# Flamingo cross-attention and expert block: whole turns of three angle chunks by matmuls, weight splits one unit later

## What is computed

```python
x = x + tanh(g_xattn) * xattn(layernorm(x), ctx, Wq, Wk, Wv, Wo, q_norm_w, k_norm_w, pos_ctx, pos_x)
x = x + tanh(g_ffn)   * ffn(layernorm(x), w_router, w_gate, w_up, w_down, ws_gate, ws_up, ws_down)
```

```python
inv_freq = 1.0 / 10000 ** (arange(0, 128, 2) / 128)
freqs = pos[..., None] * inv_freq                    # 64 angles for each position
x * cos(freqs, freqs) + rotate_half(x) * sin(freqs, freqs)
```

## Time and profile before

| | us |
|---|---|
| median of 3 runs | 1235.36 |
| lowest and highest run | 1235.15, 1236.42 |
| profiled execution | 1235.88 |
| span of its trace | 1234.10 |
| TensorE busy in the span | 1198.6 |
| DVE, ACT, POOL busy | 1015.6, 885.7, 925.6 |

### The profile page before, as it was taken

One profiled execution on the slowest core, in us unless ns is written; L12 is line 12 of the kernel. 1 busy time (PEld: TensorE's weight loads), 2 busy tenths in 40 slices (PEclk: granted clock), 3 DMA queues, 4 the chain that ended last, 5 costly groups with the idle time before them and its releaser, 6 DMA issues.

```text
span 1234.1 us, 31450 instructions
## 1 busy us (share of the span) xinstructions
PE 1198.6 (97%) x8773; PEld 1137.1 (92%) x8774; DVE 1015.6 (82%) x3003; ACT 885.7 (72%) x3756; POOL 925.6 (75%) x1118
## 2 busy tenths in 40 slices
PE   3799999999999999999999999999999999999998
PEld 1599999999999999999999999999999899999997
DVE  8899888888888888888888888888888677777443
ACT  8887777777777777777777777777777546666322
POOL 3688888888888888888888888788887526556654
PEclk8999999999999999999999999999999999999999
DMA  6624333332222232223333333322236536555574
GB/s 177 199 91 129 93 98 104 110 93 89 89 89 89 89 94 89 94 89 93 97 112 109 99 99 111 114 76 75 75 109 183 211 103 188 164 165 152 184 235 155
DMA packets 128788, 148.50 MB, mean 120 GB/s; under 512 B 13824, under 2 KB 108288, under 8 KB 127968
## 3 DMA queue, kind: packets, MB, share of 16 engines
q1 hardware_dynamic: 122256, 130.16, 35.1%
q0 software_dynamic: 6480, 17.77, 3.9%
HBM read 66.93 MB, written 80.76 MB: 120 GB/s over the span
## 4 chain that ended last, share of the span: by engine, by line
PE 94%; DVE 3%; ACT 2%; issue 1%; POOL 0%; DMA 0%; SPq 0%; DVEq 0%; POOLq 0%
PE b_kv L1681 14%; PE b_o L1762 14%; PE b_q L1667 14%; PE b_sc L1736 9%; PE b_aT L1751 9%; PE b_pT L1744 5%; PE b_qT L1725 4%; PE b_q L1980 3%; PE b_kv L1980 3%; PE b_kT L1721 2%; PE b_q L1777 2%; PE b_kT L1777 2%; PE b_aT L1895 1%; PE b_aT L1997 1%; PE b_pT L1997 1%; PE b_kT L1869 1%
## 5 line engine op out<-in xcount | busy, mean ns | idle before, releaser
L1681 PE MATMUL b_kv<-w_group,kv_in_hi 128*128 128x256 f32 x992 | 205.5, 305 | 0.2 <-DVE k_sin L1233 0.2
L731 POOL TENSOR_TENSOR qk_r<-qk_me,minus_half 128x6 f32<-128x6 f32 x128 | 174.2, 1361 | 10.0
L941 ACT ACTIVATE probs<-b_sc,neg_max 128x128 f32<-128x128 f32 x512 | 180.0, 371 | 0.3 <-DVE neg_max L1257 0.3
L735 POOL TENSOR_TENSOR q_rot<-q_rot,q_sin 128x512 f32<-128x512 f32 x128 | 165.2, 1290 | 7.1 <-DVE q_sin L1247 2.2
L1681 PEld LDWEIGHTS b_kv<-w_group,kv_in_hi 128*128 128x128 f32 x992 | 162.0, 190 | 7.0 <-issue 0.8
L1667 PE MATMUL b_q<-w_group,kv_in_hi 128*128 128x512 f32 x496 | 165.0, 414 | 0.0
L935 ACT ACTIVATE pT<-b_pT 128x512 f32<-128x512 f32 x128 | 76.6, 598 | 103.8 <-PE b_pT L1744 101.9
L1762 PE MATMUL b_o<-wo_hi,aT_hi 128*128 128x256 f32 x496 | 148.5, 299 | 0.2
L738 POOL TENSOR_TENSOR q_rot<-q_rot,qk_r 128x512 f32<-128x512 f32 x128 | 133.6, 1043 | 10.0
L1736 PE MATMUL b_sc<-kT,qT 128*128 128x128 f32 x1024 | 136.0, 276 | 4.0 <-ACT qT L930 3.9
L1681 PE MATMUL b_kv<-w_group,kv_in_lo 128*128 128x256 f32 x496 | 139.8, 282 | 0.0
(11 more groups left out here) (292 smaller groups left out, 3939.1 us busy)
## 6 DMA issues: line engine op xcount, KB each, us to landing
xs_scratch<-zeros SPq DMA_DIRECT2D x34, 1032.0 KB, 6.4
s_in<-xs_scratch SPq DMA_DIRECT2D x71, 129.0 KB
yT_scratch<-yT SPq DMA_DIRECT2D x32, 256.0 KB, 2.0
yS<-yT_scratch SPq DMA_DIRECT2D x32, 256.0 KB, 3.5
routed<-ys_scratch SPq DMA_DIRECT2D x32, 256.0 KB, 3.6
w_hi_all<-w_scratch SPq DMA_DIRECT2D x3, 1536.0 KB, 13.0
x_in<-in_x SPq DMA_DIRECT2D x32, 128.0 KB, 2.3
ctx_raw<-in_ctxT SPq DMA_DIRECT2D x32, 128.0 KB, 2.6
```

Of the source, the lines that this page charges most:

```text
L731: nc.gpsimd.tensor_tensor(qk_r[g % 2][:], qk_me[:], minus_half[:, 0:REP + NB], ALU.pow).then_inc(r_ready, 1)
L735: nc.gpsimd.tensor_tensor(q_rot[g % 2][:], q_rot[g % 2][:], q_sin[g % 2][:], ALU.add) \
L941: last = nc.scalar.activation(probs[:, j, :], b_sc[:, j * P:(j + 1) * P], ACT.Exp, bias=neg_max[g % 2][:, j:j + 1], accum_out=row_sum[g % ...
L1681: last = nc.tensor.matmul(b_kv[:, s * 2 * HD:(s + 1) * 2 * HD], kv_in[p][a][:, c, 2 * s:2 * s + 2, :], wkv_of(b, c)[:, g % KVH, :], start= ...
```

## The change

Three of the eight chunks (1, 2 and X0+2; `PE_ANGLES`) no longer have their whole turns subtracted on DVE. TensorE adds up, in one PSUM bank each, the angles times the identity and the turns times three scaled identities `back[m]`, whose diagonals are minus the three parts of 2 pi; DVE only clamps the sum out of PSUM. `angles` becomes `turn_back` (the three links) and `clamp`. The rounding of chunks 2 and X0+2 moves from ACT to DVE, that of X0+3 from DVE to ACT. TensorE's three `angle_left` stand behind `first_queries(0)` and behind `first_keys_values(0)`; `first_keys_values(1)` moves behind `heads_T(0)`. ACT's order before unit 0 changes with it. The splits move: in unit u DVE and ACT take the pieces that they took in unit u-1 before or a part of them, so that piece 8 is split in unit 5, piece 9 in 6, and pieces 10 and 11 in unit 7; the waits of TensorE for the pieces stay where they were, but that for all twelve goes to the end of unit 7.

```diff
         w_group = sb("w_group", [P, KVH, 2 * DC * (REP * HD + 2 * HD)], F32R)
+        back_at = [phase_at[0] + 4 * (KVH - 1) * 2 * DC * (REP * HD + 2 * HD)]
+        back = [sb(f"back{n}", [P, P], F32, back_at) for n in range(3)]
...
+        b_angle = (b_sc, b_pT, b_aT)
...
+        ACT_TURNS = [0, X0, 1, X0 + 1, 3, X0 + 3]
+        PE_ANGLES = [1, 2, X0 + 2]
+        turned_at, back_done = {}, {}
...
@@ gpsimd
+            for n in range(3):
+                nc.gpsimd.memset(back[n][:], 0.0).then_inc(consts_set, 1)
+            pool.wait_ge(consts_set, 12)
+            for n in range(3):
+                nc.gpsimd.affine_select(out=back[n][:], in_=back[n][:], compare_op=ALU.not_equal, fill=-TWO_PI[n], base=0,
+                                        pattern=[[-1, P]], channel_multiplier=1).then_inc(consts_set, 1)
@@ scalar
             tables(0)
             tables(X0)
-            for c in (2, X0 + 2):
-                whole_turns(c)
+            tables(1)
             query_squares(0, 0)
+            tables(X0 + 1)
             key_squares(0, 0)
             values_out(0, 0)
-            tables(1)
-            tables(X0 + 1)
-            whole_turns(3)
+            for c in (3, X0 + 3):
+                whole_turns(c)
             tables(2)
             tables(X0 + 2)
+            tables(3)
             query_squares(1, 1)
-            tables(3)
...
+                    if first and u == 0:
+                        act.wait_ge(st_trig_first, 16 * 2)
+                        queries_out(0, 0)
+                        tables(X0 + 3)
                     if not (end and g == 3):
                         key_squares(n + 1, g + 1)
-                    if first and u == 0:
-                        act.wait_ge(st_trig_first, 16 * 2)
-                    if not (first and u == 1):
+                    if not (first and u == 0):
                         queries_out(n, g)
...
+                    if first and u == 1:
+                        split_hi(pieces[0:1])
                     if first and 2 <= u < 5:
-                        split_hi(pieces[2 * u:2 * u + 2])
-                    if first and 5 <= u < 7:
-                        split_hi(pieces[5 + u:6 + u])
+                        split_hi(pieces[2 * u - 2:2 * u])
+                    if first and 5 <= u < 8:
+                        split_hi(pieces[{5: slice(8, 9), 6: slice(9, 11), 7: slice(11, 12)}[u]])
...
                     if first and u == 0:
-                        tables(X0 + 3)
                         exponent_table()
                     exponentials(n, g)
-                    if first and u < 2:
-                        split_hi(pieces[2 * u:2 * u + 2])
-                    if first and u == 0:
-                        queries_out(1, 1)
-                    else:
+                    if first and u == 1:
+                        split_hi(pieces[1:2])
+                    if not (first and u == 0):
                         attended_hi(n - 1, g - 1)
@@ vector
+            def turn_back(*chunks):
                 for part in TWO_PI:
                     for c in chunks:
-                        if part == TWO_PI[0] and CHUNKS.index(c) < 7:
-                            dve.wait_ge(turns_ready, CHUNKS.index(c) + 1)
+                        if part == TWO_PI[0]:
+                            dve.wait_ge(turns_ready, ACT_TURNS.index(c) + 1)
                         turn, a = sincos[c][:, :, 0, :], sincos[c][:, :, 1, :]
                         link(nc.vector.scalar_tensor_tensor(out=a, in0=turn, scalar=-part, in1=a, op0=ALU.mult,
                                                             op1=ALU.add), len(chunks))
...
+            def clamp(*chunks):
+                for c in chunks:
                     a = sincos[c][:, :, 1, :]
-                    nc.vector.tensor_scalar(a, a, PI_BELOW, -PI_BELOW, ALU.min, ALU.max).then_inc(angle_v, 1)
+                    if c in PE_ANGLES:
+                        n = PE_ANGLES.index(c)
+                        dve.wait_ge(count_done, n + 1)
+                        left = b_angle[n][:].rearrange("p (t n) -> p t n", t=CH)
+                    else:
+                        dve.wait_ge(step_v, back_done[c])
+                        left = a
+                    nc.vector.tensor_scalar(a, left, PI_BELOW, -PI_BELOW, ALU.min, ALU.max).then_inc(angle_v, 1)
...
             normalize_x(0, 0)
-            angles(0, X0)
+            turn_back(0, X0)
+            clamp(0, X0)
+            turn_back(X0 + 1)
             angle_products(2, X0 + 2)
-            angles(1, X0 + 1)
+            clamp(1, X0 + 1)
+            first_turns(2, X0 + 2)
             angle_products(3, X0 + 3)
...
-            angles(2, X0 + 2)
...
             turn_queries(0, 0, 0, 0)
+            clamp(2)
+            turn_back(3)
+            clamp(X0 + 2, 3)
             turn_keys(0, 0, 0)
-            first_turns(X0 + 3)
-            angles(3)
+            turn_back(X0 + 3)
+            clamp(X0 + 3)
             dve.wait_ge(st_trig_first, 16 * 2)
             keys_out(0, 0)
-            angles(X0 + 3)
...
-                    if first and u == 7:
-                        split_lo(pieces[11:12])
                     score_max(n, g)
+                    if first and u == 7:
+                        split_lo(pieces[10:11])
...
-                    if first and u == 1:
-                        split_lo(pieces[0:2])
-                        context_lo(1, 1)
...
                         normed_lo(t + 1, 1 - p)
+                    if first and u == 1:
+                        context_lo(1, 1)
...
                     if first and 0 < u < 7:
-                        split_lo(pieces[2 * u:2 * u + 2] if u < 4 else pieces[4 + u:5 + u])
+                        split_lo(pieces[2 * u - 2:2 * u] if u < 5 else pieces[3 + u:4 + u])
...
                         top_two(t - 1)
+                    if first and u == 7:
+                        split_lo(pieces[11:12])
@@ tensor
+            def angle_left(n):
+
+                c = PE_ANGLES[n]
+                if c in ACT_TURNS:
+                    pe.wait_ge(turns_ready, ACT_TURNS.index(c) + 1)
+                else:
+                    pe.wait_ge(step_v, turned_at[c])
+                turn, a = sincos[c][:, :, 0, :], sincos[c][:, :, 1, :]
+                left = b_angle[n][:]
+                nc.tensor.matmul(left, ident[:], a, start=True, stop=False)
+                for m in range(3):
+                    last = nc.tensor.matmul(left, back[m][:], turn, start=False, stop=(m == 2))
+                last.then_inc(count_done, 1)
+
             normed_x_T(0, 0)
-            for g in range(2):
-                first_queries(g)
-                first_keys_values(g)
+            first_queries(0)
+            pe.wait_ge(consts_set, 15)
+            angle_left(0)
+            first_keys_values(0)
+            angle_left(1)
+            angle_left(2)
+            first_queries(1)
...
                     heads_T(n, g)
+                    if first and u == 0:
+                        first_keys_values(1)
...
-                    if first and u == 7:
-                        pe.wait_ge(w_lo, SPLITS + 4)
                     if first and u < 2:
                         first_keys_values(u + 2)
                     elif not (end and g >= 2):
                         keys_values(n + 2, g + 2, t2, p2)
+                    if first and u == 7:
+                        pe.wait_ge(w_lo, SPLITS + 4)
```

More of the change, by code:

```diff
@@ L1175, in first_turns @@
                                                  ALU.add), len(chunks))
-            def angles(*chunks):
+                    turned_at[c] = steps[0]
+            def turn_back(*chunks):
                 for part in TWO_PI:
                     for c in chunks:
-                        if part == TWO_PI[0] and CHUNKS.index(c) < 7:
-                            dve.wait_ge(turns_ready, CHUNKS.index(c) + 1)
+                        if part == TWO_PI[0]:
+                            dve.wait_ge(turns_ready, ACT_TURNS.index(c) + 1)
                         turn, a = sincos[c][:, :, 0, :], sincos[c][:, :, 1, :]
@@ L1184, in angles @@
                                                             op1=ALU.add), len(chunks))
-                for n, c in enumerate(chunks):
-                    if n == 1:
-                        dve.wait_ge(step_v, steps[0])
+                        back_done[c] = steps[0]
+            def clamp(*chunks):
+                for c in chunks:
                     a = sincos[c][:, :, 1, :]
-                    nc.vector.tensor_scalar(a, a, PI_BELOW, -PI_BELOW, ALU.min, ALU.max).then_inc(angle_v, 1)
+                    if c in PE_ANGLES:
[6 more added lines that the diff above has]
+                    nc.vector.tensor_scalar(a, left, PI_BELOW, -PI_BELOW, ALU.min, ALU.max).then_inc(angle_v, 1)
             pieces = list(enumerate(split_pieces()))
@@ L1452, in pair @@
                         normalize_y(t - 1, 1 - p)
+                    score_max(n, g)
                     if first and u == 7:
```

(5 more changed lines are left out.)

## The result

The changed kernel takes 1237.59 us (median of 15 runs, 1236.93 to 1238.98), the kernel before 1235.77 (15 runs): ratio 1.0015, 95% interval 1.0008 to 1.0022. That is 1.8 us slower, within 0.2% of no change. I had 0.7 us faster, and a range that ended at 1237.4. The profiled execution took 1237.68 us, its span is 1235.9, against 1235.88 and 1234.1.

What follows compares the result with a forecast made beforehand. TensorE was taken to bound the kernel; 4.3 us gained early less 3.6 us lost late made 0.7 us less, a median of 1234.7 us against 1235.36, with a range from 1231.7 to 1237.4.

Steps and rivals of the forecast that it cites:

- The bound and the place: TensorE, busy 97% of the span, sets the end; the change acts only through when it begins unit 8.
- The angle matmuls cost nothing: Prologue: three `angle_left` of 3.44 us each fit TensorE's 11.9 us idle block, so free at full rate.
- `clamp(1)` at 16.2: DVE in the prologue: served at 16.2 us, after `angle_left(0)` at full rate, so its new wait costs nothing.
- my second rival: Prologue: `angle_left(0)` at half rate takes 6.9 us, so `clamp(1)` holds up DVE; 2.7 us more, 1238.1; chance 0.16.
- The third rival: Prologue: turns leave DVE but ACT's pace through the tables hides it; 3.4 us gained, 1235.6, within the forecast.
- The port collision: Prologue: DVE's `turn_back(3)` and POOL's query-half adds keep one another out; 0 to 2.4 us, taken as 1.8.
- Early gain 4.3 us: Units 0 and 1: 2.0 us by `first_queries(3)` plus the 2.5 us wait before `first_keys_values(3)`, less 0.2 for the clock.
- Late loss 3.6 us: Units 4 to 8: postponed weight splits make TensorE wait, 3.6 us by `heads_T(8)`; bounds 1.85 to 4.7.
- The waits for `wo_lo`: TensorE idle in units 6, 7 and at the start of 8, about 0.6, 1.3 and 1.7 us.
- My premise that nothing changes behind unit 7: After unit 7 the kernel waits on TensorE whatever came before, so only the start of unit 8 counts.
- My first rival: Units 6 to 8: DVE is ahead, late loss only 1.85 us, early gain kept; time 1232.0; chance 0.22.
- my own signs of being wrong: Unit 0 exponentials before 36.5 or after 39, three waits under 2 us, or `heads_T(8)` over 2 us from 98.5.

Runs made afterwards that it cites:

- run 1: Changed kernel with the split calls and TensorE's wait for all twelve pieces back where the kernel before has them; ratio 0.9999 to the kernel before.
- run 6: Two kernels with the old prologue and no angle matmuls, but `queries_out(1)` where the change has it: old splits from unit 2 0.9977, later splits 1.0012.
- run 7: Changed kernel with another order of DVE's angle work: `turn_keys(0)` and `clamp(X0+2)` ahead of `turn_back(3)`; ratio 1.0002 to the kernel before.
- 8a: The kernel of run 5 with the order of DVE's angle work of run 7; ratio 0.9966 to the kernel before.
- run 3: Changed kernel, but TensorE waits for piece 10 in unit 8 and piece 11 in unit 9, not for all twelve before `heads_T(8)`; ratio 0.9999.
- run 5: Changed kernel, but pieces 0 to 3 all split at the end of unit 1, later splits and the twelve-piece wait as in the kernel before; ratio 0.9981.
- run 4: Changed kernel with 26 transposes of the identity on TensorE ahead of its first work; ratio 1.0014 to the kernel before.
- 6a: The kernel of run 5 with the prologue of before, no angle matmuls, but `queries_out(1)` where the change has it; ratio 0.9977.
- run 8b: The kernel of run 7 with the later waits for pieces 10 and 11 of run 3; ratio 0.9987 to the kernel before.
- 6b: Kernel before with the later splits, no angle matmuls, and `queries_out(1)` on ACT where the change has it; ratio 1.0012.
- runs 2: Kernel before with only the later splits: prologue of before, no angle matmuls; ratio 1.0028 to the kernel before.

## Why the prediction was wrong

**The bound and the place** were right: TensorE carries the end, and all of the difference has arisen by unit 10.

**The angle matmuls cost nothing** by their own time: right. Three times four of them lie in the idle block; run 1 is no slower. That they bring something was wrong in the change's own order (run 6).

**`clamp(1)` at 16.2**: it came at 17.29. I took TensorE at full rate from 12.66, as the earlier trace rows had it, though my second rival named this very place. The 3.44 us that I took for half rate weren't all at that rate either: in six of the other profiles the same four records took 3.78. The rows of the changed kernel:

```profile
9.35 3.78 PE L1721 MATMUL b_q<-wq_raw,kv_first 128*128 128x512 f32 x4 [0.57 <-ACT kv_first L983]
12.92 1.76 PE L1803 MATMUL b_sc<-sincos,ident 128*128 128x512 f32 x2
14.52 2.74 PE L1805 MATMUL b_sc<-sincos,back 128*128 128x512 f32 x6
17.29 0.69 DVE L1211 TENSOR_SCALAR sincos<-b_sc 128x512 f32<-128x512 f32 x1 [1.32 <-PE b_sc L1805]
```

Two records took 1.76 us where six took 2.74, so the full rate began at about 14.5. The column of the granted clock stands at 1.00 all through 8 to 16 us, so this is read from the durations. In this profile the 1.1 us passed on whole: `turn_back(3)` at 24.92 for 23.8, the first exponentials at 39.01 for 37.9. In the other order of the DVE the link holds too: between runs 7 and 8a 0.70 us at `clamp(1)` are 0.72 at the exponentials. So the rival was true in kind, at a third of its price.

But an earlier `clamp(1)` would hardly have been enough. Runs 3 and 5 have the changed prologue with `clamp(1)` at 16.96 and 16.79, and their first exponentials stand at 39.35 and 39.20. There TensorE ran `first_keys_values(1)`, which the change puts behind `heads_T(0)`, wholly at the lower rate, and ACT waited for it (run 5):

```profile
32.92 3.62 PE L1732 MATMUL b_kv<-wkv_raw,kv_first 128*128 128x256 f32 x8
36.58 0.28 ACT L925 ACTIVATE junk<-b_kv 128x128 bf16<-128x128 f32 x1 [0.56 <-PE b_kv L1732]
```

The changed kernel's profile had 2.62 us for it and no such wait. Of the profiles with the change's order only run 4 had it at the full rate (1.89 us), and there `clamp(1)` at 15.70 gave exponentials at 37.43. I had taken 0.2 us for the clock there; the granted clock was 0.50 from 32 to 34 us.

**The third rival**, that the turns leave the DVE and the tables come no earlier, describes the first part best: the first exponentials stand at 39.01, before at 39.02. It gave 3.4 us of early gain; 3.77 were measured. I had counted it as part of the forecast, and its reason, ACT's pace, was only the last link: ACT began `tables(X0+2)` at 29.50 behind 1.45 us of waiting for the DVE.

**The port collision** was sized right: I took 1.8, and 3.82 against 2.14 for three undisturbed links is 1.7. The Trainium skill, "SBUF — State Buffer", section "SBUF: two separate sides", makes the shared ports an exclusive lock between a GpSimd operation that reads SBUF and a DVE operation with two inputs in SBUF. The trace agrees as far as it goes: POOL's two operations took 1.73 and 1.37 us beside the links, 1.27 and 1.04 in run 7, and the clamps that read PSUM took 0.68 and 0.69 us with POOL busy or idle.

**Early gain 4.3 us**: measured 3.77 at `heads_T(5)`, 0.5 short, and partly by luck. The 1.1 us before the exponentials didn't come, and at `first_queries(3)` (45.46, before 46.02) only 0.56 us of the 2.0 were there. The wait of 2.53 us went, as forecast, and 0.7 more came bit by bit up to the end of unit 4, where I had counted nothing.

**Late loss 3.6 us**: measured 4.9 by `heads_T(8)`, beyond my upper bound of 4.7. This is the step that failed. The waits for `wo_lo` were where I put them, 0.66, 0.56 and 1.97 us for 0.6, 1.3 and 1.7. What I had not in the sum were two waits for other work of the DVE that stands behind a split. By `heads_T(8)` the loss is made of 0.47 us before `scores(5)`, the three waits, 3.19, another 0.69 before `keys_values(9)`, and 0.54 in pieces that no wait names.

The first is in unit 5, and it is the price of the second piece in unit 4, for which I had 0.2. The DVE, POOL and TensorE:

```profile
72.68 0.68 DVE L1218 TENSOR_TENSOR w_group<-wkv_raw,w_group 128x512 fp32r<-128x512 f32 x1
73.28 1.22 DVE L1236 TENSOR_TENSOR kv_in_lo<-ctx_raw,kv_in_hi 128x256 fp32r<-128x256 f32 x1
74.43 0.41 DVE L1275 COPY kT<-b_kT 128x256 f32<-128x256 f32 x1
73.15 1.07 POOL L723 TENSOR_TENSOR cos_w<-trig_raw,w_cos 128x384 f32<-128x384 f32 x1
74.94 1.13 PE L1763 MATMUL b_sc<-kT,qT 128*128 128x128 f32 x8 [0.47 <-issue]
```

`scores(5)` needs the copy of the keys, which ends at 74.84. The row of L1236, the low part of the context, took 0.41 us in the kernel before; here it starts just after POOL's. In all seven profiles with the later splits it took 1.22 us and the wait is 0.46 to 0.48; in the five with the old ones (before, runs 1, 5, 6a, 8a) it took 0.41 and there is no wait.

The second is in unit 7:

```profile
92.62 0.69 DVE L1279 TENSOR_REDUCE neg_max<-b_sc 128x4 f32<-128x512 f32 x1 [1.11 <-PE b_sc L1763]
93.23 1.83 DVE L1218 TENSOR_TENSOR wo_lo<-wo_raw,wo_hi 128x1024 fp32r<-128x1024 f32 x1
...
96.21 0.34 DVE L1255 SCALAR_TENSOR_TENSOR k_sin<-b_kv,qk_r,sin_w 128x128 f32<-128x128 f32 x1
...
98.72 1.20 DVE L1218 TENSOR_TENSOR wo_lo<-wo_raw,wo_hi 128x1024 fp32r<-128x1024 f32 x1
```

```profile
91.59 1.27 POOL L748 TENSOR_TENSOR q_rot<-q_rot,q_sin 128x512 f32<-128x512 f32 x1
92.94 1.04 POOL L751 TENSOR_TENSOR q_rot<-q_rot,qk_r 128x512 f32<-128x512 f32 x1
```

The split of piece 10 starts while POOL is at L751 and takes 1.83 us, not 1.20. I had charged splits only to who waits for them; this one stands ahead of `turn_keys`, and `keys_values(9)` waits 0.92 us for those, where it waited 0.23 before. The kernel before also has a split ahead of these keys, but there it stands ahead of `score_max`, and no idle time lies between (its rows below). The change put the split behind `score_max`, so that the DVE first waits 1.11 us for the scores and splits only then:

```profile
94.19 1.21 DVE L1196 TENSOR_TENSOR wo_lo<-wo_raw,wo_hi 128x1024 fp32r<-128x1024 f32 x1
95.32 0.68 DVE L1257 TENSOR_REDUCE neg_max<-b_sc 128x4 f32<-128x512 f32 x1
```

No run moves this one call alone, so its share is read from the rows and not shown by experiment. Late keys also make the last split, at 98.72, late. The sizes of the second and third wait are off for the same reason: lateness moved from one to the next.

**After unit 8** I had nothing; 0.7 us more went between `heads_T(8)` and `heads_T(10)`. These two units took 14.48 us before and in run 5, 15.16 in the changed kernel and 15.49 in run 3. In the changed kernel 0.58 of it is in unit 9, and starts with the scaling of the probabilities at the end of unit 8, again beside POOL:

```profile
106.37 1.34 DVE L1287 TENSOR_TENSOR probs<-probs,row_inv 128x384 f32<-128x384 f32 x1
106.28 1.01 POOL L723 TENSOR_TENSOR cos_w<-trig_raw,w_cos 128x384 f32<-128x384 f32 x1
```

It took 0.61 us before. Behind it `attended_lo` ends at 108.31 and `project(7)` begins at 108.36, 0.18 late, and `normed_x_T` waits 0.3 us for the normalised x. In the seven profiles with the later splits this row took 0.97 to 1.39 us, in the other five 0.61 to 0.69. So the later splits shift the DVE against POOL, and a meeting that cost nothing before now does. My premise that nothing changes behind unit 7, where the kernel waits on TensorE anyway, was wrong by these 0.7 us. The link from this row to TensorE is read from the traces; no run isolates it.

In sum 0.5 us of the miss is the early gain, 1.3 the late loss, 0.7 what came after: 2.5, from -0.7 to +1.8. My first rival, that the gain is kept, held only in runs 5, 6a and 8a, where the splits from unit 2 on are back in their old places. Of my own signs of being wrong only one spoke, and by 0.01 us: the exponentials after 39. The three waits together were over 2 us, and `heads_T(8)` was 1.8 us off, not 2; the bounds that I had set there were too wide to catch this.

## What to carry to other kernels

Work that is moved later is not free until the last consumer's wait has been put where that consumer needs it: half of the gain here was lost at one wait that asked for all pieces together, the last of them a whole unit early. When work is put off, put it off to the next gap, not to the end of a queue (run 5 against the changed kernel, 0.34%). Charge moved work also to what stands behind it in the same queue, and look at what it will then run beside: three meetings of the DVE with POOL that no term had took part in the loss. And when a change frees an engine, look for an order in which that engine's next consumer is served first: with the same matmuls, four calls in another order on the DVE were worth about 1.5 us (runs 5 and 8a, one profile each).

## What the runs showed of the hardware

TensorE's half rate ended at another moment in each profile. With the same program up to there, the first two records of `angle_left(0)` took from 1.02 us (run 7) to 1.91 (run 1), so that the full rate began between about 12.5 and 14.7 us, and `clamp(1)` stood between 16.16 (run 8b) and 17.58 (run 1). The Trainium skill, "TensorE: Matmul & The Clock Gate", section "Part 1: The HAM clock gate (the "warmup" mystery)", calls the moment of the transition variable from run to run, since what sets it doesn't start with the kernel, and gives 500 ns to either side. The rows agree that it varies, with a wider spread of 2 us.

After idle blocks of 1.97 to 2.00 us before `heads_T(8)`, TensorE ran the next 3.5 us or so at the lower of its two levels in two profiles (runs 4 and 6b; their unit 8 took 8.9 us, not 7.33, so 1.6 us lost each) and stayed at the upper one in three others (changed, runs 2 and 7). So an idle block that looks 2 us long may cost 3.6. How often it does in the executions that weren't profiled no run shows; a median can hold both kinds.

DVE operations on two tensors in SBUF that met a POOL operation took longer in four places of the changed kernel: 3.82 us for 2.14, 1.83 for 1.20, 1.22 for 0.41, 1.34 for 0.61.
